# A four-layer graph network on one core: one-hot products for a fifth of the first layer's chunks, its edge norm by a quadratic form, its degrees by step functions

## What is computed

```python
h = relu(layernorm(x)); x = x + L0(h, edge_weight)   # mean over incoming edges
    msg = h[src] * weight[:, None]
    h_neigh = segment_sum(msg, dst) / max(deg, 1)
    h @ W_self.T + b_self + h_neigh @ W_neigh.T + b_neigh
h = relu(layernorm(x)); x = x + L1(h, edge_attr_3)   # attention per channel
    d = gelu(layer_norm(x3 @ Wd1 + bd1, g1, b1))
    d = gelu(layer_norm(d @ Wd2 + bd2, g2, b2))
    softmax over the edges of a target of (w1[dst] - w2[src] + d), times (w3[src] + d)
h = relu(layernorm(x)); x = x + L2(h, edge_attr_64)  # edge MLP with batch norm, mean, node MLP
h = relu(layernorm(x)); x = x + L3(h)                # plain sum over incoming edges
```

## Time and profile before

| what | us |
|---|---|
| timed runs: 2035.49, 2026.37, 2035.09, median | 2035.09 |
| the profiled execution's span (the whole of what it shows) | 2601.9 |
| PE / VectorE / ScalarE / GpSimd busy in it | 1601.6 / 1551.6 / 895.7 / 1327.9 |
| first gather | 27.1 |
| first layer's first and last scan | 85.4, 785.1 |
| first last row fetched | 792.9 |
| second layer's main stage | 887 to 1445 |
| end | 2601.9 |

### The profile page before, as it was taken

How to read it: one execution, slowest core, us unless ns; L and a number is a source line. 1 busy time by engine, 2 the same in 40 slices (tenths; PEclk the granted TensorE clock), 3 DMA queues, 4 the chain that set the end, 5 groups by cost and what they waited for, 6 DMA issues and landing times.

```text
span 2601.9 us, 23168 instructions
## 1 busy us (share of the span) xinstructions
PE 1601.6 (62%) x6953; PEld 1209.1 (46%) x6953; DVE 1551.6 (60%) x2430; ACT 895.7 (34%) x1175; POOL 1327.9 (51%) x1397
## 2 busy tenths in 40 slices
PE   1546554555565655555665247888786725889892
PEld 1334433443354444444453235666565514767672
DVE  5445545554477477677776635554555934868783
ACT  1222222222231755555553113332333811433340
POOL 6555555455534455555664455446551036656554
PEclk8566666666676777787787568898897657989896
DMA  6111211121121344444444313323224602333332
GB/s 141 36 51 54 63 52 51 53 63 52 52 68 54 99 142 145 139 141 147 145 146 129 83 37 70 69 59 75 65 65 101 204 13 53 85 78 84 78 79 57
DMA packets 223807, 219.66 MB, mean 84 GB/s; under 512 B 108066, under 2 KB 170967, under 8 KB 223447
## 3 DMA queue, kind: packets, MB, share of 16 engines
q1 hardware_dynamic: 175575, 147.75, 19.3%
q0 software_dynamic: 44384, 56.98, 10.5%
q10 hardware_dynamic: 3744, 13.63, 1.3%
HBM read 116.77 MB, written 101.46 MB: 84 GB/s over the span
## 4 chain that ended last, share of the span: by engine, by line
PE 23%; another core or an unknown queue 13%; issue 11%; DVE 11%; ACT 5%; POOL 3%; DMA 2%; SPq 1%; DVEq 0%; POOLq 0%; ACTq 0%
PE psum L993 16%; POOL arena L676 3%; PE psum L1018 1%; DVE scan_ring L1935 1%; DVE spare L1935 1%; DMA maxima<-arena 1%; DVE arena L1810 1%; PE psum L1085 1%; ACT spare L1257 1%; DVE arena L1816 1%; PE psum L1024 1%; ACT spare L1331 1%; DMA keep<-keep_rows 1%; DVE spare L1760 1%
## 5 line engine op out<-in xcount | busy, mean ns | idle before, releaser
L636 POOL DMA_INDIRECT gathered<-table,idx x1264 | 1208.6, 956 | 1014.9 <-issue 363.6
L1760 DVE COPY_PREDICATED spare<-spare,psum 64x512 f32<-64x512 uint8 x300 | 220.8, 736 | 303.7 <-ACT spare L1355 208.2
L993 PE MATMUL psum<-rounded 128*128 128x512 f32 x1144 | 303.8, 419 | 63.8 <-issue 43.4
L993 PEld LDWEIGHTS psum<-rounded 128*128 128x128 f32 x1144 | 227.3, 202 | 124.9 <-issue 59.2
L780 PE MATMUL psum<-ident,arena 128*128 128x128 f32 x416 | 107.9, 409 | 287.5 <-ACT arena L1140 272.1
L1592 DVE TENSOR_REDUCE rs<-arena 128x16 f32<-128x1024 f32 x52 | 63.4, 1219 | 302.3 <-ACT arena L1144 249.6
L780 PEld LDWEIGHTS psum<-ident,arena 128*128 128x128 f32 x416 | 69.8, 205 | 354.9 <-ACT arena L1140 284.0
L1144 ACT ACTIVATE arena<-psum 128x1024 f32<-128x1024 f32 x52 | 53.3, 1025 | 410.9 <-remote 280.3
L1355 ACT ACTIVATE spare<-psum 64x512 f32<-64x512 f32 x82 | 48.5, 592 | 397.7 <-remote 199.0
L676 POOL DMA_INDIRECT arena<-scan,rowidx x75 | 79.3, 1058 | 206.7 <-DMA scan<-ea 114.3
L906 PE MATMUL psum<-ident,arena 128*128 128x128 f32 x172 | 34.4, 335 | 189.3 <-ACT arena L1246 185.5
(11 more groups left out here) (285 smaller groups left out, 3444.9 us busy)
## 6 DMA issues: line engine op xcount, KB each, us to landing
scan<-ostage SPq DMA_DIRECT2D x130, 256.0 KB, 2.3
scan<-arena SPq DMA_DIRECT2D x52, 512.0 KB
gathered<-table,idx POOLq DMA_INDIRECT x1264
d_mlp<-arena ACTq DMA_DIRECT2D x26, 512.0 KB
arena<-d_mlp SPq DMA_DIRECT2D x52, 256.0 KB
maxima<-arena SPq DMA_DIRECT2D x52, 256.0 KB
ea<-in_edge_attr SPq DMA_DIRECT2D x104, 128.0 KB
spare<-src_row SPq DMA_DIRECT2D x100, 128.0 KB
```

What stands on the lines that cost most here:

```text
L636: pool.indirect_dma_start(out=out[:, j, hf, :], out_offset=None, in_=tab[layer], in_offset=bass.IndirectOffsetOnAxis(ap=idx[:, j, hf * NCH ...
L993: last = nc.tensor.matmul(P[:, bank + t, :], parts[layer][n][:, b:b + 2, :].rearrange("p b d -> p (b d)"), tile(layer, m, u)[:, hf * CH:(h ...
L1760: picked = v.copy_predicated(rows[m % 2][halves[hf], :], quarter[m % 2][halves[hf], q - 1, :], P[halves[q % 2], bank + q // 2, :])
```

## The change

1. `MULTIPLIED[0]` holds ten chunks (6, 11, ..., 51). Their rows come from one-hot products (`l0_multiply`, L908), spread over the chunks before in four parts; one-hots by ScalarE for three of seven groups and by VectorE (L1826) for four, picks L1814, and a product with the edge weights (L1835), which SP loads broadcast. 336 gathers are left. The node table is split into its two parts before the first scan (`split_table(0, ...)`).
2. The first norm of the edge MLP: the variance of `x3 @ Wd1 + bd1` over channels is a quadratic form in (x3, 1). Its matrix is made from the centred weights, factored, and evaluated for all edges at once on 104x512 tiles; the attributes times the reciprocal root are split in three bf16 parts, stored to DRAM (6 DMAs) and loaded again for each pair (`load_attrs`, 3 DMAs). The body then has one bf16 product of 88 rows for each chunk (`l0_mlp1`, L824) whose result goes straight into the first GELU. `Wd1` is loaded by 24 small DMAs instead of 9, and two more load a copy for the matrix.
3. The degrees: instead of a histogram, for each block of 128 nodes two bf16 products of 426 columns (`l0_count`, L834) with step functions lay out, for each node of the block, the row of `dst` in which its edges end, and VectorE counts in that row (`l0_counted`, L1805, L1807). This is done in chunks 2 to 26, and `rowidx` is made in chunks 27 to 30, inside the loop.
4. All of the first layer is written out chunk by chunk; no engine has a loop there.

```diff
-MULTIPLIED = {1: list(range(1, NCH - 1, 6)), 2: [n * NCH // 19 for n in range(19)], 3: [c for c in range(NCH) if c % 12 in (0, 2, 5, 7, 9)]}
+MULTIPLIED = {0: list(range(6, NCH, 5)), 1: list(range(1, NCH - 1, 6)), 2: [n * NCH // 19 for n in range(19)], 3: [c for c in range(NCH) if c % 12 in (0, 2, 5, 7, 9)]}
...
+            def load_attrs(i):
+                if i >= 3:
+                    sp.wait_ge(S("mlp1 made"), 2 * (i - 3) + 2)
+                for n in range(NPARTS):
+                    sp.dma_start(xs[i % 3][n * 32:n * 32 + AROWS, :], attr_dram[:, i * 2 * CH:(i + 1) * 2 * CH]) \
+                        .then_inc(S("attrs loaded", i % 3), 16)
...
+            def l0_mlp1(i, k):
+                n = 2 * i + k
+                if k == 0:
+                    pe.wait_ge(S("attrs loaded", i % 3), NPARTS * 16 * (i // 3 + 1))
+                if n:
+                    pe.wait_ge(S("gelu1 made"), n)
+                if COUNTED < n <= COUNTED + NB:
+                    pe.wait_ge(S("blocks counted"), n - COUNTED)
+                if n == 29:
+                    pe.wait_ge(*stage("rowidx made"))
+                if n == 31:
+                    pe.wait_ge(*stage("rows indexed"))
+                rows_in = (NPARTS - 1) * 32 + AROWS
+                nc.tensor.matmul(P[:, 0, :], w1p[0:rows_in, :], xs[i % 3][0:rows_in, k * CH:(k + 1) * CH],
+                                 start=True, stop=True).then_inc(S("mlp1 made"), 1)
...
+            def l0_count(c):
+                b = c - COUNTED
+                pe.wait_ge(S("gelu1 made"), c + 1)
+                if b == 0:
+                    pe.wait_ge(*stage("count operands made"))
+                for n, diff in enumerate((diff_hi, diff_lo)):
+                    last = nc.tensor.matmul(P[:, 0, 0:HC + 1], steps_up[0:HR, b * 128:(b + 1) * 128], diff[0:HR, 0:HC + 1],
+                                            start=(n == 0), stop=(n == 1))
+                last.then_inc(S("block chosen"), 1)
...
+            for c in range(NCH):
+                i, k = c // 2, c % 2
+                if c in FETCHED[0]:
+                    l0_in(c)
+                l0_mlp1(i, k)
+                if k == 0:
+                    if c:
+                        l0_out(i - 1, 1)
+                        l0_norm_transpose(i - 1, 0)
                 else:
-                    pe.wait_ge(S("gelu made"), past(g))
-                pe.wait_ge(S("norms1 made"), i + 1)
-                norm_transpose(0, 0)
-                l0_in(i, 0)
-                if more:
-                    mlp1_products(i + 1)
-                pe.wait_ge(S("gelu made"), past(g + 1))
-                norm_transpose(0, 1)
-                if not first:
-                    l0_out(i - 1, 1)
-                pe.wait_ge(S("gelu made"), past(g + 2))
-                if not first:
-                    pe.wait_ge(S("norms2 made"), past(i))
-                    norm_transpose(1, 0)
-                l0_in(i, 1)
-                if not first:
-                    pe.wait_ge(S("gelu made"), past(g + 3))
-                    norm_transpose(1, 1)
-                if more:
-                    mlp2_products()
-                l0_hist(i)
-                l0_out(i, 0)
-            pe.wait_ge(*stage("edge attrs copied"))
-            x3_transposes(0)
-            mlp1_products(0, first=True)
-            l0_body(0, first=True)
-            for i in range(1, NIT - 1):
-                l0_body(i)
-            l0_body(NIT - 1, more=False)
+                    if i:
+                        l0_norm_transpose(i - 1, 1)
+                    l0_mlp2(i)
+                    l0_out(i, 0)
+                if COUNTED <= c < COUNTED + NB:
+                    l0_count(c)
+                l0_ends(c)
+                if c == 0:
+                    pe.wait_ge(*stage("h0 split"))
+                l0_multiply_after(c)
...
+            step(v.tensor_tensor(gram_terms, attr_w[:, :, :].unsqueeze(2).to_broadcast([128, NA, NA, D]),
+                                 attr_w[:, :, :].unsqueeze(1).to_broadcast([128, NA, NA, D]), ALU.mult))
+            flat = gram[:, :, :].rearrange("p a b -> p (a b)")
+            step(v.reduce_sum(flat, gram_terms.rearrange("p a b d -> p (a b) d"), axis=AX))
...
+            dve.wait_ge(S("attr rows loaded"), 32)
+            step(v.scalar_tensor_tensor(combo1, x3[:, 1, :], coefficient(0, 0), x3[:, 0, :], ALU.mult, ALU.add))
+            step(v.scalar_tensor_tensor(combo1, x3[:, 2, :], coefficient(0, 1), combo1, ALU.mult, ALU.add))
+            step(v.scalar_tensor_tensor(combo2, x3[:, 2, :], coefficient(1, 0), x3[:, 1, :], ALU.mult, ALU.add))
+            dve.sem_inc(stage_of("attr combos made"), 1)
+            l0_message(1)
+            dve.wait_ge(*stage("attr squares made"))
+            step(v.tensor_scalar(variance, combo1, pivot[0:NROW, 0:1], pivot[0:NROW, 3:4], ALU.mult, ALU.add))
+            step(v.scalar_tensor_tensor(variance, combo2, pivot[0:NROW, 1:2], variance, ALU.mult, ALU.add))
+            step(v.scalar_tensor_tensor(variance, square3, pivot[0:NROW, 2:3], variance, ALU.mult, ALU.add))
+            rsqrt_of(variance, attr_r[:, 3, :], combo1, step, tuned=True)
+            for n in range(3):
+                step(v.tensor_tensor(attr_r[:, n, :], x3[:, n, :], attr_r[:, 3, :], ALU.mult))
+            for n in range(NPARTS):
+                step(v.tensor_copy(attr_parts[:, n, :, :], attr_r))
+                if n + 1 < NPARTS:
+                    step(v.tensor_tensor(attr_r, attr_r, attr_parts[:, n, :, :], ALU.subtract))
+            dve.sem_inc(stage_of("attr parts made"), 1)
...
+            def l0_counted(c):
+                b = c - COUNTED
+                dve.wait_ge(S("block chosen"), b + 1)
+                v.tensor_scalar(below[:, 0:HC], P[:, 0, 0:HC], tally[:, 2, b:b + 1], None, ALU.is_le, ALU.add,
+                                accum_out=tally[:, 1, b:b + 1])
+                v.tensor_copy(tally[:, 0, b:b + 1], P[:, 0, HC:HC + 1]).then_inc(S("blocks counted"), 1)
...
+            def l0_picks_after(c):
+                for hf, ahead in ((0, 4), (1, 1)):
+                    if c + ahead in MULTIPLIED[0]:
+                        m = MULTIPLIED[0].index(c + ahead)
+                        pick(0, m, hf, (1, 7))
+                        if hf == 1:
+                            weighted(m)
+            def l0_onehots_after(c):
+                for u, ahead in ((0, 10), (2, 9), (4, 7), (6, 6)):
+                    if c + ahead in MULTIPLIED[0]:
+                        make_onehots(0, MULTIPLIED[0].index(c + ahead), (u,))
...
+            for c in range(-10, 0):
+                l0_onehots_after(c)
+            for c in range(NCH):
+                if c == NFIRST:
+                    dve.wait_ge(S("keep loaded"), 32)
+                l0_scan(c)
+                if c and c % 2 == 0:
+                    norms2(c // 2 - 1)
+                l0_picks_after(c)
+                l0_onehots_after(c)
+                if COUNTED <= c < COUNTED + NB:
+                    l0_counted(c)
+                l0_ends(c)
+                if c + 2 in FETCHED[0]:
+                    l0_message(c + 2)
+            norms2(NIT - 1)
```

More of the change, by code:

```diff
@@ L1180, in _ @@
[L1180 to L1187 removed]
+            act.wait_ge(*stage("attr combos made"))
+            x3 = ea3_rows.rearrange("p (e a) -> p a e", a=3)
+            for n, (dst, src) in enumerate(((combo1, combo1), (combo2, combo2), (square3, x3[:, 2, :]))):
+                last = nc.scalar.activation(dst, src, ACT.Square, bias=lower[0:NROW, n, NA - 2 - n:NA - 1 - n])
```

777 lines of the change are left out of this document (439 added, 338 removed).

## The result

The changed kernel takes **2090.35 us** (median of 4 runs, 2087.44 to 2095.54), the kernel before in the same comparison 2030.73 (2025.58 to 2035.49): ratio 1.0294, interval 1.0258 to 1.0331. That is 59.6 us more; forecast were 62, and 2097 us.

What follows compares the result with a forecast made beforehand. GpSimd's gathers were taken to bound the first layer (20.05 us a pair, last scan at 558). After: start-up 97 plus TensorE's chain 525 gives 622; less 2 at the tail, +62 on 2035 makes 2097 us, range 1980 to 2165.

Steps and rivals of the forecast that it cites:

- late releases: Waits in the profile before whose releaser it can't name: 227 us in the first layer, 336 behind, absent from timed runs.
- Gathers left out: First layer, GpSimd: 10 of 52 chunks not gathered, 100 us less, giving nothing beyond the point where TensorE's chain binds.
- The start-up: Before the first scan: new work item by item, 53.6 us, VectorE ready at 97 where the scan was at 58; bounds 30 and 55.
- the weights' wait: Start-up: weights arrive 7 us later, as 26 small loads stand on SP where 9 stood, 0.34 each.
- TensorE's chain: First-layer loop after: 18.9 us a pair at full clock, taken as 20.8; 26 pairs less savings make 525 us.
- the hole: TensorE idle in each even chunk before the norm transposes, for scan and norm: 5.6 us, or 4 to 5 in the signs.
- The rule 18.9 / g: Pair time at granted clock g if slow stretches all carried work: 18.9 at 1, 23.6 at 0.80; 0.91 taken, 20.8.
- The tail: After the last scan: row indices are ready earlier, so last rows start sooner, 2 us off, between 0 and 5.
- later layers: Layers after the first keep their work, only semaphore and buffer names change: nothing.
- A: Rival, faster: late releases are real in timed runs of the looped first layer and go; 1987 us if half are; chance 0.30.
- B: Rival, slower still: granted clock 0.80 through TensorE's holes, pairs of 23.6 us, total 2170; chance 0.12.
- C: Rival, no difference: TensorE keeps the full clock, total 2047, or 2038 with the start-up at its lower bound; chance 0.12.

Runs made afterwards that it cites:

- before_again: The kernel before, unedited, profiled once more: 2035.0 us in one run, span 2033.3.
- before_table_late_2: The kernel before with 16 loads of later layers' weights put ahead of the node table's store, run again: 2039.49 us against 2028.48, ratio 1.0047.
- no_multiplied: The changed kernel with no multiplied chunk in the first layer, all 52 gathered: 2077.01 us, ratio 1.0236 to the kernel before.
- wd_on_act: The changed kernel with its 24 small loads of Wd1 issued by ScalarE's queue instead of SP's: 2072.05 us, ratio 1.0218 to the kernel before.
- six_multiplied: Changed kernel, second norm moved to odd chunk's end, Wd1 loads on ScalarE's queue, six multiplied chunks: 2507.16 us, ratio 0.9604 to before; run again 2005.52, 0.9886.

## Why the prediction was right, and where it was off

**What bounds the kernel before.** Right. The prediction took the late releases out of the trace (227 us in the first layer, 336 behind it) and put GpSimd's 16 gathers in the place of TensorE's 18.4 us. Between the two profiles of before it is 234 and 334. before_again shows the pair of 20.0 us and the last scan at 550.92 (558 predicted); before_table_late_2 shows that a first gather 9.9 us later ends the program 9.5 us later.

**Gathers left out give nothing by themselves.** Right: no_multiplied is not slower than the change, by ratio and last scan 8 to 12 us faster.

**The start-up, +39.** The step and its sign are right, its size is 48.8, inside the bounds of 30 and 55. Of the 10 us too little, 4 are that before's first scan was taken at 58 and stands at 54.03, and 6 that after's is at 102.85 instead of 97. By item: the weights' wait is the one that was mis-sized most. It was priced at 7 us, 0.34 for a small load from a row of another shape; the loads took 0.69, VectorE went on at 38.38 instead of 23.09 with 4 us of its index work already done, 11 us. wd_on_act took out 13. The matrix (6.5 for 5.7), combinations to products (14 with the wait for ScalarE's squares, for 13), parts (8.4 for 8.5), split (5.1 for 5.3) and one-hots (3.6 for 3.8) fit. The parts' trip through DRAM, put beside the split, does delay TensorE's first product, to 105.08, but behind the first scan, so that this cost lies in the loop's 501.0.

**TensorE's chain, 525 us against 500.** The mechanism is right (the hole of 4.94 us, released by the norm's product), the size too high by 24: 501.0, and 496.9 for before. The pair was taken as 20.8 less 0.6 for what some chunks lack, 20.2, and is 19.7 on average. That is 14 of the 24; the other 10 are that 26 pairs were counted, where 25 and a half lie between the first scan and the last. The rule 18.9 / g would give 22.5 at the granted 0.84 of the stage, and the pairs are shorter, but not because the slow stretches are idle. By the granted clock in half microseconds, TensorE is at its lower level for some 159 of the 501 us and busy in about 119 of them; at the full clock that work would take some 59 us less, an estimate, 2.3 a pair, where the step from 18.9 to 20.8 had counted 1.9. So the clock's term is about right, and the sum at the full clock is too large, 17.3 by this estimate for 18.3. Which of its terms is too large no run isolates. A hint is no_multiplied, whose first five pairs take 16.3 us at a granted 0.73: against the average of 19.7 the multiplies add 3.4 a pair, where 4.56 were put on top in full.

**The tail, -2.** Wrong sign, +3.0: the fetch of last rows now waits for the last scan's store. Measured less forecast is -21 for the loop, +10 for the start-up, +5 for the tail and +4 for later layers, which were put at nothing: these nearly cancel, so that 62 against 60 is partly luck.

**The rivals.** A was tested by before_again and falls: none of the measured 2030 us is a late release. The Trainium skill's rule on taken branches ("Runtime: NRT & Kernel Launch", section "Instruction fetch mechanics") changes nothing here either: before_again runs the old loops on ScalarE and VectorE, and its pairs are 20.0 us with no gap at the branch that reaches GpSimd; how long a stall at the branch is, no run here shows. B: the clock of the stage was 0.84, nearer to B's 0.80 than to 0.91, without B's time. C needed the full clock throughout and a start-up at its lower bound; it was 0.84 and 48.8 us.

**What was not tried.** Norm 1 and the counts were not undone one by one in the new body; the first layer's start-up was shortened by one item only. The parts' trip through DRAM was not taken out either. How the changed kernel compares in executions with late releases is open; six_multiplied gained 103 us on before there and 23 without them.

## What to carry to other kernels

Before a unit's work is taken off, ask which chain is next and how far below it stands: here a chain of 18.4 us stood under 20.05, and after the change the chain takes 19.7, and gathers left out in that order gave nothing. Where an in-order engine has a block of 5 us that others wait for, the place of the block in its queue is worth more than the work saved: moving it to where VectorE was idle brought the last scan 71 us forward and turned the multiplied chunks, which had gained nothing, into a gain of 59 us. Work done once for all edges is paid before the first scan, at its full price, when nothing of the loop can run beside it.

## What the hardware showed that was not expected

The kernel before took 2610.56 us in one job and 2028.48 in a later one on the same chip. The profiles of the first job have TensorE's completions late throughout (8 us in the rows of six_multiplied above), those of the second have none. What makes them late was not found.

A small load of one source row to three partitions that lie eight apart took 0.69 us of SP's queue, and 0.34 where three rows of the source went to three partitions side by side. That the source is broadcast isn't enough to explain it: the two loads of the copy for the matrix, broadcast to 128 partitions, took 0.42 and 0.41.

```profile
34.11 0.42 SPq L463 DMA_DIRECT2D attr_w<-in_L_gnn_Wd  x1
```

A gather, 0.94 us elsewhere, took up to 3.28 us while VectorE made the parts (no_multiplied, and after as well).
